# Loading expert weights in sixteen pieces inside the attention loop instead of two large transfers ahead of it

## The chip, the cores and the metric

The kernel runs on one core of one Trainium2 chip. The metric is the device time of one execution in microseconds (us), as the median of several runs.

## What is computed

One transformer block over 2048 tokens of width 128, in float32: an adaptive layer norm, sparse attention with 16 heads of 8 columns in which each head attends only to its 819 best-scored keys (40% of 2048), a second layer norm, and a feed-forward layer with 8 experts, of which each token uses one. Cut to what matters here:

```python
ga = (2 * (ga >= 0) - 1) * jnp.maximum(jnp.abs(ga), 0.25)        # gb likewise
h = _layernorm(x) * (1 + ca) + sa
x = x + ga * attention(h)          # per head: the top 819 keys by a routing score, softmax, weighted sum of values
h = _layernorm(x) * (1 + cb) + sb
logits = jnp.einsum('btd,ed->bte', h, router_w)
mask = jax.nn.one_hot(jnp.argmax(jax.nn.softmax(logits), axis=-1), 8)
u = jnp.square(jax.nn.relu(jnp.einsum('btd,edh->ebth', h, expert_fc)))
out_e = jnp.einsum('ebth,edh->ebtd', u, expert_proj)
x = x + gb * jnp.einsum('ebtd,bte->btd', out_e, mask)
```

The weights of the experts, `expert_fc` and `expert_proj`, are 2 MB each. They are used in the second half alone.

## The kernel before

Every engine has its own program, written out by hand, and semaphores order them; nothing is scheduled by a tool. The engines are PE (tensor engine: matmuls and transposes), DVE (vector engine), ACT (scalar engine), POOL (general engine) and SP, which here only issues transfers.

First the layer norm, the projections and the choice of keys for each head. A table of positions is built for this on DVE (lines 1000 and 1005). Its first stage, `B0`, lies in the memory that later holds the expert weights, `WE`, so the weights may only come in once the first five tables are done; SP waits for that on the semaphore `columns_ready`.

Then the attention loop. Heads go in 8 pairs, and each pair's 2048 queries in 4 chunks of 512, so there are 32 chunks, `n` = 0 to 31. Per chunk:
- PE makes scores for the maxima of a later chunk, in "units" of 128 queries by about 410 keys (lines 1437 to 1442), and DVE reduces each unit to its maximum (line 1067). The maxima are split into three bfloat16 parts (lines 1077 to 1084), PE turns them (`turn_m`, line 1456), ACT copies them to `MT` (line 764), and SP moves them with two small transfers, one for each head of the pair, into three rows of `QS` under the queries (`m_rows`, line 484). In this way the maxima are subtracted inside the score matmul. Each such transfer adds 16 to the semaphore `mrow`.
- PE starts a chunk only when its own rows are there: `pe.wait_ge(mrow, 32 * (n + 1))` on line 1543. It then makes the scores in seven steps (`scores`, line 1485), ACT takes the exponential of each step (line 791), and PE weighs the values with them (`weigh`, line 1501).
- The rows of chunk `n + 1` are turned in step 3 of chunk `n`, so their transfer is issued in the second half of chunk `n`.

At the head of every fourth chunk SP also loads the queries of the pair after the next (`load_q`, line 476, six transfers). POOL meanwhile gathers the keys and values of a coming pair from memory (line 562) and prepares them (lines 579 to 611); PE turns the prepared keys (`turn_k`, line 1450).

After the loop come the second layer norm, the routing, the sorting of tokens by expert, and 23 tiles of 128 tokens. For each tile DVE copies one expert's two weights out of `WE` (lines 1285 and 1291). Before the first of these copies it waits on `we_in`, the semaphore of the weight transfers.

All transfers that SP issues go through one queue. The part of it that the change touches:

```python
m_rows(0)
sp.wait_ge(columns_ready, AHEAD)
for n, w_part in enumerate((w_fc, w_proj)):
    sp.dma_start(WE[:, :, HD * n:HD * (n + 1)], w_part.rearrange("n p c -> p n c"))\
        .then_inc(we_in, 16)
for n in range(NCH):
```

Of the kernel before, what the change touches and what calls it, by code (L numbers as in the profile page):

```python
# [95 lines left out]
NE = 8  # L96
HD = 4 * E
# [56 lines left out]

def build(nc, x, w_q, w_kv, b_q, b_kv, w_r1, b_r1, w_r2, b_r2, c_col, wmod, w_route, w_fc, w_proj, const, out):
    _, at = constants()
    NCONST = const.shape[1]
    q_parts_dram = nc.dram_tensor("q_parts_dram", (H, PARTS, D, L), BF16, kind="Internal").ap()
# [3 lines left out]
    with ExitStack() as ctx:  # L162
        def sb(name, shape, dt=F32):
            return ctx.enter_context(nc.sbuf_tensor(name, shape, dt))
# [4 lines left out]
        def sem(name):  # L169
            return ctx.enter_context(nc.semaphore(name))  # L170
# [34 lines left out]
        WE = sb("WE", [P, NE, 2 * HD])  # L205
# [141 lines left out]
        we_in = sem("we_in")  # L347
# [104 lines left out]
        @block.sync  # L452
        def _(sp):
            for g in range(4):
                sp.dma_start(X[:, 4 * g:4 * g + 4, :], x_t[:, 4 * g:4 * g + 4, :]).then_inc(x_in[g], 16)
                if g == 1:
                    sp.dma_start(C[:, :], const).then_inc(const_in, 16)
            for dst, src in ((WR1, w_r1), (WR2S, w_r2), (BR1, b_r1), (BR2, b_r2), (WQ, w_q), (WKV, w_kv), (BQ, b_q),
                             (WROUTE, w_route)):
                sp.dma_start(dst[:, :], src).then_inc(w_in, 16)  # L460
            sp.dma_start(BG[:, :, :, :], b_kv).then_inc(bias_in, 16)

            for g in range(4):
                sp.wait_ge(kv_ready, 2 * g + 2)
                sp.dma_start(kv_t[:, 4 * g:4 * g + 4, :], KV[:, 4 * g:4 * g + 4, :]).then_inc(kv_out, 16)
            for part in range(PARTS):
                sp.wait_ge(q_ready, 4 * part + 4)
                sp.dma_start(q_parts_dram[:, part, :, :], QP[:, part, :]).then_inc(qparts_out, 16)
            sp.wait_ge(qparts_out, 16 * PARTS)
            sp.wait_ge(qs_zero, 2)  # L470

            def load_q(i):
                for e in range(2):
                    src = q_parts_dram[2 * i + e:2 * i + e + 1, :, :, :].rearrange("h a d l -> (h a d) l")
                    for row, k in ((0, 3), (3, 2), (5, 1)):
                        sp.dma_start(QS[64 * e + D * row:64 * e + D * (row + k), i % 2, :],
                                     src[0:D * k, :]).then_inc([qs_even, qs_odd][i % 2], 16)

            def m_rows(n):
                c = n % NQ  # L480
                sp.wait_ge(mt_ready, n + 1)
                for e in range(2):
                    dst = QS[64 * e + KROWS:64 * e + SROWS, n // NQ % 2, CHUNK * c:CHUNK * (c + 1)]
                    sp.dma_start(dst.rearrange("a (t q) -> a t q", q=P), MT[12 * e:12 * e + 12, n % 2, :])\
                        .then_inc(mrow, 16)

            load_q(0)
            load_q(1)
            m_rows(0)
            sp.wait_ge(columns_ready, AHEAD)  # L490
            for n, w_part in enumerate((w_fc, w_proj)):
                sp.dma_start(WE[:, :, HD * n:HD * (n + 1)], w_part.rearrange("n p c -> p n c"))\
                    .then_inc(we_in, 16)
            for n in range(NCH):
                if n % NQ == 0 and 1 <= n // NQ < NP - 1:
                    sp.wait_ge(st_filled, KSTEPS * n)
                    load_q(n // NQ + 1)
                if n + 1 < NCH:
                    m_rows(n + 1)


            for g in range(4):
                ts = slice(4 * g, 4 * g + 4)
                sp.wait_ge(x2_ready, 2 + g)
                sp.dma_start(rows_t[:, ts, E:2 * E], X2[:, ts, :]).then_inc(rows_out, 16)
                sp.wait_ge(xn2_ready, 4 * g + 4)
                sp.dma_start(rows_t[:, ts, 0:E], XN2[:, ts, :]).then_inc(rows_out, 16)
            sp.wait_ge(added, 16 * SLOT_TILES)
# [350 lines left out]
        def _(dve):  # L859
# [412 lines left out]
            dve.wait_ge(tail_step, next_tail())  # L1272
            v.scalar_tensor_tensor(owner[:, :], OWNER, -1.0, empty[:, :], ALU.add, ALU.add).then_inc(owner_ready, 1)  # L1273
            dve.wait_ge(tile_ready, 1)
            dve.wait_ge(we_in, 32)

            expert_reg = [dve.alloc_register("expert_even"), dve.alloc_register("expert_odd")]

            def load_expert(n):
                dve.reg_load(expert_reg[n % 2], TEI[0:1, n:n + 1])  # L1280
# [411 lines left out]
```

## Time and profile before

| | us |
|---|---|
| median of 3 timed runs | 525.98 |
| the three runs | 526.09, 525.98, 523.41 |
| span of the profiled execution, first to last instruction | 558.4 |
| busy in it: PE, DVE, ACT, POOL | 451.8, 396.4, 311.3, 217.7 |

The profiled execution has no time of its own besides its span, and the span is 32.4 us above the timed median; the rows and sums that follow are of the profiled execution. In the rows, PE is the tensor engine's matmuls, PEld its loading of the stationary operand (which runs beside PE), SPq the issuing of transfers by SP. `QS<-MT` is the transfer of the rows of maxima, `WE<-in_w_fc` and `WE<-in_w_proj` are the expert weights. A time in square brackets at a row's end is how long the engine stood idle before it, and what ended the idle time.

### The profile page before, as it was taken

How to read it: one execution, taken by the hardware profiler on the slowest of the kernel's cores; microseconds unless marked ns; L12 is line 12 of the kernel's file. 1: busy time of each engine (PE TensorE's matmuls, PEld its weight loads, DVE VectorE, ACT ScalarE, POOL GpSimd, SP SyncE). 2: the span in 40 equal slices, each digit the busy share in tenths (PEclk: the TensorE clock that was granted, in tenths of full speed). 3: DMA queues.
4: the chain of work that ended last, by engine and by line, in shares of the span. 5: the costliest groups of instructions: out<-in, count | busy, mean ns of one | idle time of the engine just before them, and what ended most of it. 6: DMA issues, size and time to landing. Idle time of an engine off the chain costs nothing.

```text
span 558.4 us, 9397 instructions
## 1 busy us (share of the span) xinstructions
PE 451.8 (81%) x3252; PEld 221.0 (40%) x3253; DVE 396.4 (71%) x1063; ACT 311.3 (56%) x457; POOL 217.7 (39%) x301
## 2 busy tenths in 40 slices
PE   4674754789999997998999899999999770769665
PEld 4341621223433432443434333333333270658564
DVE  8788864758986996787689668888889558134323
ACT  3435000357785785676578567778778740446333
POOL 3100576523414375266248425442003000655643
PEclk9878555569997999999799989999999955788878
DMA  7034300620100100100010010010000040211100
GB/s 230 0 126 118 82 6 6 217 90 4 32 2 6 33 3 5 30 6 6 3 32 3 6 32 2 6 33 2 2 2 0 22 133 0 76 41 42 44 17 12
DMA packets 20207, 21.11 MB, mean 38 GB/s; under 512 B 5740, under 2 KB 15792, under 8 KB 20160
## 3 DMA queue, kind: packets, MB, share of 16 engines
q1 hardware_dynamic: 14704, 16.12, 9.6%
q0 software_dynamic: 5168, 4.00, 3.9%
q8 instruction: 26, 0.43, 0.3%
q10 hardware_dynamic: 288, 0.39, 0.2%
q14 instruction: 21, 0.17, 0.1%
HBM read 14.41 MB, written 7.27 MB: 39 GB/s over the span
## 4 chain that ended last, share of the span: by engine, by line
PE 67%; DVE 16%; issue 7%; another core or an unknown queue 3%; DMA 2%; ACT 2%; POOL 1%; SPq 0%; POOLq 0%; DVEq 0%; ACTq 0%
PE OP L1501 17%; PE ST L1485 13%; PE ST L1461 6%; PE SC L1439 6%; PE SC L1437 6%; DVE tile_max L1067 5%; PE SC L1620 4%; PE ST L1631 3%; DVE PR L937 2%; PE OP L1509 2%; PE SC L1391 2%; DMA QS<-MT 2%; PE OP L1586 1%; PE SC L1441 1%
## 5 line engine op out<-in xcount | busy, mean ns | idle before, releaser
L1067 DVE TENSOR_REDUCE tile_max<-SC 128x1 f32<-128x410 f32 (+1 forms) x512 | 271.4, 577 | 74.9 <-PE SC L1437 49.2
L791 ACT ACTIVATE PR<-ST 128x1024 f32<-128x1024 f32 (+1 forms) x224 | 208.7, 962 | 62.4 <-PE ST L1485 57.0
L562 POOL DMA_INDIRECT G<-kv_dram,idx x104 | 106.8, 1027 | 169.0 <-ACT PR L791 108.8
L1485 PE MATMUL ST<-QS,KT 51*128 51x512 bf16 (+1 forms) x416 | 112.8, 403 | 3.6 <-DMA QS<-MT 2.7
L1501 PE MATMUL OP<-PR,VS 128*32 128x512 f32 x768 | 111.2, 653 | 0.4 <-ACT PR L791 0.4
L1437 PE MATMUL SC<-KT,QS 48*128 48x410 bf16 x256 | 80.6, 370 | 8.5 <-DVE tile_max L1067 4.5
L1485 PEld LDWEIGHTS ST<-QS,KT 51*128 51x128 bf16 (+1 forms) x416 | 30.2, 97 | 55.5 <-issue 39.3
L1439 PE MATMUL SC<-KT,QS 48*128 48x409 bf16 x128 | 47.3, 370 | 4.0 <-DVE tile_max L1067 1.1
L1441 PE MATMUL SC<-KT,QS 48*128 48x358 bf16 x128 | 43.4, 339 | 5.8 <-DVE tile_max L1067 3.7
L1620 PE MATMUL SC<-HT,PR 128*128 128x128 f32 x184 | 29.9, 316 | 18.3 <-issue 15.7
L686 POOL DMA_INDIRECT KV<-rows_dram,owner x23 | 24.3, 1054 | 50.5 <-DVE owner L1273 43.8
L1291 DVE COPY PR<-WE 128x512 f32 x23 | 10.4, 451 | 41.6 <-PE ST L1631 22.6
L838 ACT ACTIVATE HT<-ST,mod_col,one_cb 128x128 f32<-128x128 f32 x23 | 10.5, 457 | 52.1 <-PE ST L1611 31.2
L1461 PE MATMUL ST<-C,OS 128*128 128x32 f32 x248 | 38.8, 281 | 0.2
L1437 PEld LDWEIGHTS SC<-KT,QS 48*128 48x128 bf16 x256 | 19.3, 96 | 46.4 <-DVE tile_max L1067 30.4
L764 ACT ACTIVATE MT<-ST 24x128 bf16<-24x128 bf16 x32 | 8.5, 267 | 50.7 <-PE ST L1461 22.3
L1461 PEld LDWEIGHTS ST<-C,OS 128*128 128x128 f32 x248 | 32.2, 190 | 11.4 <-issue 10.7
L1620 PEld LDWEIGHTS SC<-HT,PR 128*128 128x128 f32 x184 | 27.1, 227 | 20.0 <-issue 17.0
L1439 PEld LDWEIGHTS SC<-KT,QS 48*128 48x128 bf16 x128 | 12.0, 94 | 57.5 <-DVE tile_max L1067 41.8
L695 POOL DMA_INDIRECT out<-PR,owner x23 | 23.3, 1015 | 26.6 <-DVE PR L1299 20.7
L618 POOL TENSOR_TENSOR XN<-OTS,REC 128x128 f32<-128x128 f32 x14 | 5.5, 413 | 61.2 <-DVE REC L1090 56.4
L1631 PE MATMUL ST<-PR 128*128 128x128 f32 x184 | 27.9, 300 | 0.3 <-issue 0.3
(257 smaller groups left out, 555.2 us busy)
## 6 DMA issues: line engine op xcount, KB each, us to landing
kv_dram<-KV SPq DMA_DIRECT2D x4, 512.0 KB, 2.9
WE<-in_w_fc SPq DMA_DIRECT2D x1, 2048.0 KB
WE<-in_w_proj SPq DMA_DIRECT2D x1, 2048.0 KB
G<-kv_dram,idx POOLq DMA_INDIRECT x104
q_parts_dram<-QP SPq DMA_DIRECT2D x3, 512.0 KB, 3.7
QS<-q_parts_dram SPq DMA_DIRECT2D x16, 96.0 KB
X<-in_x SPq DMA_DIRECT2D x4, 256.0 KB, 6.1
QS<-q_parts_dram SPq DMA_DIRECT2D x16, 64.0 KB
```

The lines of the kernel that those rows point to most:

```text
L562: pool.indirect_dma_start(G[:, i % 2, slot_of(s), :], None, kv_dram, bass.IndirectOffsetOnAxis(ap=idx[:, i, s:s + 1].bitcast(U32), axis=0) ...
L686: pool.indirect_dma_start(HS[:, n % NT, :], None, rows_dram, bass.IndirectOffsetOnAxis(ap=owner[:, n:n + 1].bitcast(U32), axis=0), bounds_ ...
L791: nc.scalar.activation(PR[:, k, 0:cols], ST[:, (KSTEPS * n + k) % 2, 0:cols], ACT.Exp, scale=float(D) ** -0.5).then_inc(exp_done, 1)
L1067: v.tensor_reduce(tile_max[:, n % 2, at_col:at_col + 1], bank(RING_AT["unit", u])[:, 0:410 - f], AX.X, ALU.max).then_inc(s_reduced, 1)
L1437: last = mm(to[:, 0:410], q, KT[rows, i % 2, 0:410], start=True, stop=True)
L1439: last = mm(to[:, 0:409], q, KT[rows, i % 2, 410:KEEP], start=True, stop=True)
L1441: mm(to[:, 0:358], q, KT[rows, i % 2, 410:768], start=True, stop=True)
L1461: last = mm(turned_o(n)[:, 32 * t:32 * t + 32], OS[:, P * t:P * t + P], cc("sum_groups"), start=True, stop=True)
L1485: last = mm(ST[:, at_step % 2, 512 * e:512 * e + 512], KT[rows, i % 2, P * tile:P * tile + P], QS[rows, i % 2, CHUNK * c:CHUNK * (c + 1)], ...
L1501: last = mm(OP[32 * g:32 * g + 32, :], VS[:, i % 2, tile, :], PR[:, k, 512 * e:512 * e + 512], start=first, stop=False, skip_group_check=True)
L1620: last = mm(SC[:, b, P * c:P * c + P], WFC[:, b, P * c:P * c + P], HT[:, P * n:P * n + P], start=True, stop=True)
L1631: last = mm(ST[:, b, 0:E], R2[:, b, P * c:P * c + P], WPROJ[:, b, P * c:P * c + P], start=(c == 0), stop=(c == 3))
```

## The change

The two transfers of 2 MB ahead of the loop go. In the loop, each of the chunks 0 to 15 issues one transfer of 256 KB (one expert's half: up or down projection) right after it has issued the rows of maxima of the next chunk. The wait for `columns_ready` stays where it was. DVE waits for sixteen landings instead of two.

```diff
             m_rows(0)
             sp.wait_ge(columns_ready, AHEAD)
-            for n, w_part in enumerate((w_fc, w_proj)):
-                sp.dma_start(WE[:, :, HD * n:HD * (n + 1)], w_part.rearrange("n p c -> p n c"))\
-                    .then_inc(we_in, 16)
+
+            def load_expert(piece):
+                at, half = piece // 2, piece % 2
+                sp.dma_start(WE[:, at, HD * half:HD * (half + 1)], (w_fc, w_proj)[half][at]).then_inc(we_in, 16)
+
             for n in range(NCH):
                 if n % NQ == 0 and 1 <= n // NQ < NP - 1:
                     sp.wait_ge(st_filled, KSTEPS * n)
                     load_q(n // NQ + 1)
                 if n + 1 < NCH:
                     m_rows(n + 1)
-
+                if n < 2 * NE:
+                    load_expert(n)
...
-            dve.wait_ge(we_in, 32)
+            dve.wait_ge(we_in, 16 * 2 * NE)
```

On SP's queue, at the start of the chunk loop, the order of issues changes as follows (`QS<-MT` is a pair of row transfers where it says x2, `QS<-q_parts_dram` are loads of queries, a count stands behind x):

```order
 L476 DMA QS<-q_parts_dram 16x2048
 L476 DMA QS<-q_parts_dram 8x2048
+L484 DMA QS<-MT 3x4x128 x4
+L494 DMA WE<-in_w_fc 128x512
 L484 DMA QS<-MT 3x4x128 x2
-L492 DMA WE<-in_w_fc 128x8x512
-L492 DMA WE<-in_w_proj 128x8x512
-L484 DMA QS<-MT 3x4x128 x8
+L494 DMA WE<-in_w_proj 128x512
+L484 DMA QS<-MT 3x4x128 x2
```

The rows of chunks 0 and 1 now follow each other directly, and the first piece of a weight stands behind the rows of chunk 1, the second behind those of chunk 2.

Further on in the loop, SP's queue over chunks 4 to 7, between two sets of query loads, shows what is new in a later group of chunks:

```order
 L476 DMA QS<-q_parts_dram 8x2048
-L484 DMA QS<-MT 3x4x128 x8
+L484 DMA QS<-MT 3x4x128 x2
+L494 DMA WE<-in_w_fc 128x512
+L484 DMA QS<-MT 3x4x128 x2
+L494 DMA WE<-in_w_proj 128x512
```

Four pairs of rows that stood in one run now each have a piece behind them. The order of the instructions on PE, DVE, ACT and POOL is the same in both kernels.

## Rows read from the trace of the kernel before

**Rows 1.** The page: span, and the chain that ended last by engine.

```profile
span 558.4 us, 9397 instructions
...
PE 67%; DVE 16%; issue 7%; another core or an unknown queue 3%; DMA 2%; ACT 2%; POOL 1%; SPq 0%; POOLq 0%; DVEq 0%; ACTq 0%
```

**Rows 2.** The chain, 96 to 135 us: start us, us, what.

```profile
100.79 1.85 DMA QS<-MT
...
102.69 0.95 PE ST L1485 x2
...
107.76 0.73 SPq L484
...
108.53 6.79 DMA QS<-MT
115.32 0.68 issue
116.00 1.25 PE ST L1485 x3
```

**Rows 3.** SP's timeline, 97 to 112 us.

```profile
101.58 0.42 SPq L492 DMA_DIRECT2D WE<-in_w_fc  x1
102.06 0.57 SPq L492 DMA_DIRECT2D WE<-in_w_proj  x1
107.76 1.47 SPq L484 DMA_DIRECT2D QS<-MT  x2
```

**Rows 4.** Stretches: us, busy us of each engine, clock share, DMA share, GB/s.

```profile
core 0: us, PE busy (x) PEld busy (x) DVE busy (x) ACT busy (x) POOL busy (x), PEclk, DMA share, GB/s
104.00:114.00 10.00, 9.88 (x52) 2.43 (x50) 7.73 (x18) 6.46 (x8) 3.05 (x3) 0.50 1.02 372
114.73:116.00 1.27, 0.00 (x1) 0.00 (x1) 0.00 (x0) 0.00 (x0) 0.96 (x1) 0.50 0.22 72
116.00:119.84 3.84, 3.84 (x19) 1.08 (x21) 2.06 (x4) 2.03 (x3) 0.15 (x1) 0.50 0.04 2
119.84:123.25 3.41, 3.04 (x25) 1.94 (x21) 2.88 (x8) 2.94 (x4) 0.85 (x1) 1.00 0.04 5
123.25:126.67 3.42, 3.42 (x19) 0.79 (x19) 1.15 (x3) 1.45 (x3) 1.00 (x1) 0.50 0.03 4
126.67:129.09 2.42, 2.42 (x24) 0.62 (x22) 2.40 (x5) 2.01 (x2) 0.28 (x1) 1.00 0.00 0
157.54:167.81 10.27, 9.79 (x86) 3.95 (x83) 8.84 (x21) 8.28 (x11) 1.85 (x3) 1.00 0.01 2
```

**Rows 5.** PE's timeline where chunk 0 ends and chunk 1 starts.

```profile
112.80 1.93 PE L1501 MATMUL OP<-PR,VS 128*32 128x512 f32 x8
116.00 0.61 PE L1485 MATMUL ST<-QS,KT 51*128 51x512 bf16 x1 [1.27 <-DMA QS<-MT]
```

**Rows 6.** ACT's and DVE's timeline, 97 to 128 us.

```profile
112.91 1.02 ACT L791 ACTIVATE PR<-ST 128x1024 f32<-128x1024 f32 x1 [0.74 <-PE ST L1485]
127.02 1.02 ACT L791 ACTIVATE PR<-ST 128x1024 f32<-128x1024 f32 x1 [1.62 <-PE ST L1485]
...
112.58 1.07 DVE L1067 TENSOR_REDUCE tile_max<-SC 128x1 f32<-128x409 f32 x2 [0.34 <-PE SC L1442]
```

**Rows 7.** SP: its waits (us, times, longest), and its timeline from 241 us.

```profile
SPq L484 <- ACT MT L764: 256.4, 26, 38.2
...
241.56 36.56 SPq L484 DMA_DIRECT2D QS<-MT  x8
```

**Rows 8.** DMA issues: count, size of each, median us to landing.

```profile
rows_dram<-X SPq DMA_DIRECT2D x4, 256.0 KB, 2.8
```

**Rows 9.** SP's and PE's timeline around the starts of chunks 2 and 4.

```profile
129.09 0.39 PE L1485 MATMUL ST<-QS,KT 51*128 51x512 bf16 x1
...
144.22 1.44 SPq L484 DMA_DIRECT2D QS<-MT  x2
146.89 2.24 SPq L476 DMA_DIRECT2D QS<-q_parts_dram  x6
...
148.06 0.39 PE L1485 MATMUL ST<-QS,KT 51*128 51x512 bf16 x1
```

**Rows 10.** POOL's, SP's and PEld's timeline around the last gather of pair 3.

```profile
195.31 1.00 POOL L562 DMA_INDIRECT G<-kv_dram,idx  x1 [0.96 <-ACT PR L791]
198.93 0.62 POOL L579 TENSOR_TENSOR G<-G,BG 128x208 f32<-128x208 f32 x1 [2.63 <-DMA G<-kv_dram,idx]
...
195.69 1.48 SPq L484 DMA_DIRECT2D QS<-MT  x2
...
202.95 0.24 PEld L1450 LDWEIGHTS SC<-identb,KS 128*128 128x128 bf16 x4 [0.58 <-POOL RS L596]
```

**Rows 11.** Line 1285, the copies out of the expert weights.

```profile
L1285 DVE COPY PR<-WE x23: 419/422/654, 473.2 to 547.6; 128x512 f32 x23
```

## The prediction

> **What bounds the kernel now.** I read the chain that ended last first. Two thirds of it is the tensor engine [rows 1], so a change matters only where that engine is made to wait or let go earlier. The change touches one queue, SP's, so I then followed the chain in order of time over the start of the chunk loop. Here the reader is to see one piece that is out of line: the row transfer of chunk 0 takes 1.85 us from its issue to its landing, the one of chunk 1 takes 6.79, and both are followed directly by the tensor engine's score matmuls [rows 2]. SP's own timeline says why: between the two pairs of row transfers it issues the two weight transfers of 2 MB, at 101.58 and 102.06 [rows 3]. The table of stretches says that from 104 to 114 us the 16 DMA engines are full (share 1.02, 372 GB/s) [rows 4]. So the rows of chunk 1, issued behind them from 107.76, land only when the 4 MB are through, at 108.53 + 6.79 = 115.32.
>
> What that costs is read from the tensor engine alone. Its last work of chunk 0, the weighing of line 1501, starts at 112.80 and lasts 1.93, to 114.73; the first score matmul of chunk 1 starts at 116.00, with 1.27 us of idle time put down to the row transfer [rows 5]. In those 1.27 us no engine but POOL does anything [rows 4]: the last exponential of chunk 0 has ended at 112.91 + 1.02 = 113.93 and the last maximum at 112.58 + 1.07 = 113.65 [rows 6], so both wait for the tensor engine and nothing else holds chunk 1 back.
>
> **The base of the sum.** The profiled execution spans 558.4 us, 32.4 us more than the timed median of 525.98. The rows do not say where those 32.4 us lie. I make the sum in microseconds against the span and subtract the same number from 525.98, because the wait is the difference between a transfer's landing and the end of one chunk, both near 115 us; what that choice can cost stands among the rivals.
>
> **Part 1: the 4 MB leave the place ahead of the loop.** The second row transfer of chunk 1 is then issued about 108.53 as before, on an empty queue. Chunk 0's took 1.85 us [rows 2], so it lands near 110.4, 4.3 us before the tensor engine asks at 114.73. The wait goes as a whole: -1.27 us. It is not refilled at that spot, since exponentials and maxima are done 0.8 and 1.1 us before 114.73.
>
> How much of 1.27 reaches the end depends on the clock. The tensor engine runs at the lower of its two levels, 1.2 GHz (0.50), through chunk 0 and the first 3.84 us of chunk 1; it then has 3.41 us at 2.4 GHz (1.00), 3.42 at 1.2 and is back at 2.4 [rows 4]. If the clock rises as long after the start of chunk 1 as now, the whole 1.27 is kept. If it rises at the same time of the execution as now, 1.27 us more of chunk 1 run at half speed, and the gain is 0.64. These are the two ends for this term; I take 1.27, because the rise comes after the tensor engine resumes and not before, though it had been busy for nearly all of 104 to 114 (9.88 of 10.00 us).
>
> Does chunk 0 also get faster without the transfer beside it? The exponential of 128x1024 takes 1.02 us at 112.91 under full DMA and 1.02 at 127.02 without [rows 6]. I take nothing.
>
> **Part 2: sixteen pieces of 256 KB, each behind a pair of row transfers.** SP has the time: it spends 256.4 us waiting for the copied maxima [rows 7], and a weight issue takes 0.42 to 0.57 us [rows 3]. A piece moves in 262144 B / 372 GB/s = 0.70 us at the rate of rows 4, and a 256 KB transfer of this kernel lands 2.8 us after its issue [rows 8]. The next rows come one chunk later, about 10 us (chunk 5 spans 10.27) [rows 4], so a piece has left the queue long before. The piece stands behind its own rows, never ahead of them. How tight those rows are: for chunk 4 the pair is issued from 144.22 for 1.44 us, hence the second at about 144.94, landing near 146.8 by the 1.85 of rows 2, and the tensor engine needs it at 148.06 [rows 9]: 1.26 us to spare. Between nothing and 0.70 us of sharing, both inside 1.26, I take nothing. The six loads of q at the head of every fourth chunk follow a piece by several microseconds (146.89 in rows 9) and are not needed at once.
>
> The gathers on POOL use the same 16 DMA engines. The last gather of pair 3 is issued at 195.31, its preparation starts at 198.93 after a wait of 2.63 us, and the tensor engine's transposes wait for its end until 202.95 [rows 10]. This is the one tight place. Bounds: nothing, if the gather lands before the piece moves, and 0.7 us, once, if it gives way to a whole piece. The rows of that chunk go out from 195.69 for 1.5 us, so the piece is issued near 197.2, when the gather is nearly in. I take nothing.
>
> **Part 3: the later end of the weights.** The last piece goes out behind the rows of chunk 16, in an SP run of four pairs that ends at 241.56 + 36.56 = 278.12 [rows 7]; the first read of the weights is at 473.2 [rows 11]. The cover is some 195 us, and the larger count that is waited for costs nothing.
>
> **Sum.** -1.27 + 0 + 0 = -1.3 us. On the span 557.1; on the timed median 525.98 - 1.3 = 524.7. Its own range, by the clock (-0.64) and by a timed execution whose chunk 0 runs 526/558 as long (12.04 becomes 11.35, so the wait is 2.0): 524.0 to 525.3. That is 0.25%, about half of the 0.5% that a measurement of this kernel can tell from no change (its three runs lie 2.7 us apart).
>
> **The rivals.**
> *B, the clock comes back with the wait (faster).* Chunk 1 takes 129.09 - 116.00 = 13.09 us, of which 7.26 at 1.2 GHz; chunk 5, with the same transposes of keys but wholly at 2.4, takes 10.27 [rows 4, 9]. Were chunk 1 like chunk 5, another 2.8 us come back: 525.98 - 1.27 - 2.82 = 521.9. For it: the rise does follow the resumption. Against it: 12 busy microseconds of chunk 0 raised nothing, and the clock falls again inside chunk 1 with no wait of this kind. I give it 0.17. The Trainium skill (TensorE: Matmul & The Clock Gate, HAM oscillation — how this bites in real kernels) holds that waits for transfers between bursts of matmuls put the engine back to its slow clock and that work fed without such waits keeps it fast; by that rule B would be the forecast, 521.9 in place of 524.7. The trace agrees in part: the rise follows the end of the wait, but the low stretch before it held no such waits.
>
> *C, the wait is longer when nothing is profiled (faster).* If chunk 0 took chunk 5's 10.27 us in a timed execution instead of 102.69 to 114.73 = 12.04 [rows 2, 5], the tensor engine would arrive 1.8 us earlier against the same landing, and 1.27 + 1.77 = 3.04 us would go: 522.9. Nothing shown speaks for that clock there: 0.09.
>
> *D, the clock stays low longer (slower).* Chunk 1's 3.41 us at 2.4 GHz hold 3.04 us of tensor work, which at 1.2 GHz costs 3.04 more; a further chunk like chunk 0 instead of chunk 5 costs 1.8. -1.27 + 3.04 + 1.77 = +3.5: 529.5. It decides against the change when more than 1.27 us of work that now runs at 2.4 GHz falls back to 1.2: 0.06.
>
> *E, the rows land late behind pieces (slower).* If a row pair shared the queue such that it came 2.8 us later, 1.5 us would stand open in each of the 16 chunks: +25 - 1.3, some 550. It decides from 1.26 us of delay on. Against it: the rows go first, and the previous piece is some 10 us older. I give it 0.04. The Trainium skill (DMA: Bandwidth & Descriptors, Bandwidth) speaks against small transfers, asking for 1 MiB or more in each; by the fixed 2.0 us and 436 GB/s of its anatomy section, a piece is an estimated 2.6 us, near the row's 2.8, and would be hidden too.
>
> *F, nothing to see.* The gain is eaten by the tight gather or by later changes of the clock: 526.0. Against it stands only how small 1.3 us is: 0.11.
>
> **Numbers.** The forecast holds 0.53. Faster by over 0.5%: B and C, 0.26. Slower: D and E, 0.10. Within: the rest, 0.64. The range goes down to B, 521.8, and up past F by half the spread of the three runs, 527.3; D and E and the far tails are left out.
>
> **What would show it.** In the changed profile the rows of chunk 1 land about 1.9 us after their issue, the tensor engine goes from line 1501 of chunk 0 to line 1485 of chunk 1 without idle time, and no chunk up to 16 shows a new wait for the row transfer; DMA shows a short burst in each of these chunks. Step 1 is wrong if a wait for an exponential or a maximum stands at that spot; step 2, if waits for rows appear in chunks 2 to 16 or the transposes of pair 3 wait longer than 0.6 us. A time below 523 says that the clock moved; one above 528, that chunks were held up.

## The result: 0.73% faster, by more than forecast and by another wait

The changed kernel takes 520.1 us (median of 20 runs) beside 524.38 us for the kernel before (20 runs, timed together with it): a ratio of 0.9927 with a 95% interval of 0.9908 to 0.9947, so 2.8 to 4.8 us less. The ratios leave out executions over 1.5% above the fastest of their kernel, so they are not exactly the quotient of the two medians. The forecast was 1.3 us less, with 521.8 as the lower end of its range. The direction was right, the size was about three times as large, and the time lies below the range.

One plain fact has to stand first, since the forecast can't be understood without it: the execution from which [rows 1 to 11] were taken was a disturbed one. In all later profiles the span is about 1.8 us under the time of the same run, so a span of 558.4 us belongs to a run of some 560 us. Of the 20 runs only one, of 563.17 us, is anywhere near; the other 19 lie between 520 and 529.

The page of the changed kernel has a span that fits its time (this run took 519.37 us), and the same shares by engine as [rows 1], but POOL now has 6% of the chain:

```profile
span 517.6 us, 9413 instructions
...
PE 66%; DVE 16%; issue 7%; POOL 6%; DMA 3%; ACT 1%; POOLq 0%; DVEq 0%; ACTq 0%
```

SP's timeline of the changed kernel, against [rows 3]: the rows of chunks 0 and 1 go out in one run, the first piece behind them, and each later pair has a piece behind it.

```profile
92.05 9.45 SPq L484 DMA_DIRECT2D QS<-MT  x4
101.55 0.42 SPq L494 DMA_DIRECT2D WE<-in_w_fc  x1
112.60 1.46 SPq L484 DMA_DIRECT2D QS<-MT  x2
114.10 0.42 SPq L494 DMA_DIRECT2D WE<-in_w_proj  x1
```

The chain of the changed kernel, 85 to 130 us, is where the surprise stands. Where [rows 2] had a transfer of rows, the chain now runs through POOL: its last gather for head pair 1 lands 2.42 us after its issue, is prepared (lines 582 to 614; each number is 3 higher than in the kernel before), and the first weighing of chunk 0 follows at once.

```profile
93.72 2.42 DMA G<-kv_dram,idx
...
96.21 0.64 POOL G L582
...
100.56 0.20 POOL VS L614
...
100.90 1.94 PE OP L1504 x8
```

At the start of chunk 1, which answers to [rows 5], the tensor engine's timeline shows no idle time between the last weighing of chunk 0 and the first scores of chunk 1, as forecast:

```profile
105.16 1.07 PE L1504 MATMUL OP<-PR,VS 128*32 128x512 f32 x8
106.16 0.39 PE L1488 MATMUL ST<-QS,KT 51*128 51x512 bf16 x1
```

And the stretches that answer to [rows 4] (the columns are the same): chunk 0 at the lower clock, 1.37 us of it at the higher, and chunk 1 whole at the higher in 10.27 us.

```profile
94.84:104.79 9.95, 9.40 (x47) 2.80 (x49) 7.32 (x17) 5.74 (x7) 6.35 (x18) 0.50 0.09 30
104.79:106.16 1.37, 1.37 (x14) 0.26 (x11) 1.15 (x3) 0.92 (x2) 1.07 (x2) 1.00 0.08 6
106.16:116.43 10.27, 9.79 (x85) 3.96 (x83) 8.52 (x20) 8.41 (x12) 3.55 (x5) 1.00 0.14 31
```

By these alone it could be that the wait is gone and the clock came back. So the first need was an ordinary profile of the kernel before.

### The profile page after: what moved, and what is told of

Its sections match the earlier page's. It is cut to its first block, busy times and chain, and to the rows that moved or that the text cites. A ratio compares the mean times of both kernels' runs of the same rounds, so it can differ in the third digit from the quotient of the medians.

```text
span 517.6 us, 9413 instructions
## 1 busy us (share of the span) xinstructions
PE 440.4 (85%) x3253; PEld 213.0 (41%) x3253; DVE 395.7 (76%) x1063; ACT 311.1 (60%) x457; POOL 216.9 (42%) x301
## 4 chain that ended last, share of the span: by engine, by line
PE 66%; DVE 16%; issue 7%; POOL 6%; DMA 3%; ACT 1%; POOLq 0%; DVEq 0%; ACTq 0%
PE OP L1504 19%; PE ST L1488 12%; PE ST L1464 7%; PE SC L1442 6%; DVE tile_max L1070 5%; PE SC L1440 4%; POOL G L565 4%; PE ST L1634 3%; PE SC L1623 3%; PE OP L1512 2%; DMA KV<-rows_dram,owner 2%; DVE PR L940 2%; PE OP L1589 1%; PE ST L1394 1%; PE ST L1459 1%
## 5 line engine op out<-in xcount | busy, mean ns | idle before, releaser
L1070 DVE TENSOR_REDUCE tile_max<-SC 128x1 f32<-128x410 f32 (+1 forms) x512 | 271.1, 576 | 54.9 <-PE SC L1440 51.6
L565 POOL DMA_INDIRECT G<-kv_dram,idx x104 | 105.5, 1015 | 148.5 <-ACT PR L794 88.7
L1488 PE MATMUL ST<-QS,KT 51*128 51x512 bf16 (+1 forms) x416 | 109.3, 401 | 1.8 <-DMA QS<-MT 1.5
L1504 PE MATMUL OP<-PR,VS 128*32 128x512 f32 x768 | 108.8, 640 | 0.7 <-ACT PR L794 0.4
L1464 PEld LDWEIGHTS ST<-C,OS 128*128 128x128 f32 x248 | 32.2, 190 | 11.4 <-issue 10.7
L1623 PE MATMUL SC<-HT,PR 128*128 128x128 f32 x184 | 25.9, 288 | 0.0
L1634 PE MATMUL ST<-PR 128*128 128x128 f32 x184 | 25.1, 279 | 0.4 <-issue 0.4
L1445 PE MATMUL SC<-KT,QS 48*128 48x51 bf16 x128 | 24.6, 192 | 0.0
```

Of the source, the lines that this page charges most:

```text
L565: pool.indirect_dma_start(G[:, i % 2, slot_of(s), :], None, kv_dram, bass.IndirectOffsetOnAxis(ap=idx[:, i, s:s + 1].bitcast(U32), axis=0) ...
L1070: v.tensor_reduce(tile_max[:, n % 2, at_col:at_col + 1], bank(RING_AT["unit", u])[:, 0:410 - f], AX.X, ALU.max).then_inc(s_reduced, 1)
L1464: last = mm(turned_o(n)[:, 32 * t:32 * t + 32], OS[:, P * t:P * t + P], cc("sum_groups"), start=True, stop=True)
L1488: last = mm(ST[:, at_step % 2, 512 * e:512 * e + 512], KT[rows, i % 2, P * tile:P * tile + P], QS[rows, i % 2, CHUNK * c:CHUNK * (c + 1)], ...
L1504: last = mm(OP[32 * g:32 * g + 32, :], VS[:, i % 2, tile, :], PR[:, k, 512 * e:512 * e + 512], start=first, stop=False, skip_group_check=True)
L1623: last = mm(SC[:, b, P * c:P * c + P], WFC[:, b, P * c:P * c + P], HT[:, P * n:P * n + P], start=True, stop=True)
```

## The experiments

Three theories stood: **Q**, the rows of chunk 1 stand behind the 4 MB in SP's queue (the forecast's wait, larger than it looked); **S**, the 4 MB share the 16 DMA engines with POOL's last gathers of pair 1, whose preparation the first weighing waits for; **L**, the gain lies in other stretches. They were timed in four sets, each on a chip of its own with the kernel before beside it, whose medians lay between 524.3 and 525.2 us; runs of different sets are compared by their ratios.

| run | median, us | ratio to the kernel before (95%) | from the issue of chunk 0's rows to its first weighing, us |
|---|---|---|---|
| before, second profile | 525.26 | 1.0007 (0.9969 to 1.0045) | 13.2 |
| before, third profile | 524.81 | 1.0021 (0.9985 to 1.0057) | 13.4 |
| changed, the result above | 520.1 | 0.9927 (0.9908 to 0.9947) | 8.9 |
| changed, again | 520.37 | 0.9921 (0.9877 to 0.9965) | 8.9 |
| 2 x 2 MB behind the rows of chunk 1 | 521.1 | 0.9896 (0.9838 to 0.9954) | 8.7 |
| 2 x 2 MB on ACT's queue | 524.49 | 0.9984 (0.9948 to 1.002) | 12.7 |
| 2 x 2 MB behind the loop's rows | 518.47 | 0.9856 (0.9805 to 0.9907) | 8.8 |
| the same, again | 519.88 | 0.9903 (0.9871 to 0.9934) | 8.8 |
| sixteen pieces ahead of the loop | 520.92 | 0.9942 (0.9901 to 0.9982) | 10.1 |
| 2 x 2 MB after pair 1's gathers landed | 527.5 | 1.0073 (1.0036 to 1.0109) | 8.7 |
| 2 x 2 MB ahead of the rows of chunk 0 | 520.85 | 0.9967 (0.9928 to 1.0007) | 8.8 |
| 1 MB ahead of the loop, 3 MB behind it | 522.54 | 1.0004 (0.9965 to 1.0043) | 11.8 |
| changed, POOL held up 4.2 us | 523.77 | 0.9996 (0.9962 to 1.0029) | 12.8 |

The last column is the start of the first weighing (line 1501 in the kernel before) minus the start of SP's first row issue of chunk 0, both from the run's profile. In the first profile it was 8.4 us. The edits shift the line numbers in some runs: the weighing is line 1501, 1502, 1504 or 1511.

### The kernel before, profiled again

No edit.

> The kernel before, unchanged, for a second profile of it, since the first one spans 558.4 us and the timed median is 524.4. Theory Q (queue): the rows of chunk 1 stand behind the 4 MB in SP's queue, and what that costs the tensor engine at the start of chunk 1 is larger in an ordinary execution than the 1.27 us read from the first profile: 3 to 4 us of wait there, and the lower clock lasts beyond it. Theory S (shared engines): the wait there is 1.3 us or less, and the 4 MB instead delay POOL's last gathers of pair 1 by 2 us or more, so that the first weighing of chunk 0 waits for POOL. Theory L (elsewhere): neither is above 1.3 us, and the 4 us lie in other stretches of the clock. All: 524 us, ratio 1.00.

Its profile, of a run of 528.99 us, showed the wait of S (4.78 us at the first weighing) and none of Q (the scores of chunk 1 start with no idle time before them):

```profile
106.19 1.93 PE L1501 MATMUL OP<-PR,VS 128*32 128x512 f32 x8 [4.78 <-POOL VS L611]
...
112.61 0.60 PE L1485 MATMUL ST<-QS,KT 51*128 51x512 bf16 x1
```

Since that run was one of the longer ones, a third was taken:

> The kernel before once more, for a third profile, since the second one was of one of its longer executions. Theory S: the last gather of pair 1 lands 4 to 7 us after its issue and the first weighing of chunk 0 waits 2.5 us or more for POOL; the rows of chunk 1 are not waited for. If the second profile was the exception: the gather lands within 3 us. 524 to 525 us.

The third is of a run of 520.2 us and shows the same. POOL's timeline: the last gather is issued at 93.77, its data are waited for until 100.80, and the preparation ends with line 611 at 105.33. PE's timeline: the scores of chunk 0 start at 94.95, the first weighing only at 105.47, after 4.90 us of idle time put down to POOL, and chunk 1 starts at 110.56 with no wait at all.

```profile
93.77 1.00 POOL L562 DMA_INDIRECT G<-kv_dram,idx  x1 [0.30 <-issue]
100.80 0.62 POOL L579 TENSOR_TENSOR G<-G,BG 128x208 f32<-128x208 f32 x1 [6.03 <-DMA G<-kv_dram,idx]
...
105.14 0.19 POOL L611 COPY VS<-G 64x8 f32<-64x8 f32 x1
...
94.95 0.60 PE L1485 MATMUL ST<-QS,KT 51*128 51x512 bf16 x1 [1.52 <-DMA QS<-MT]
105.47 1.94 PE L1501 MATMUL OP<-PR,VS 128*32 128x512 f32 x8 [4.90 <-POOL VS L611]
...
110.56 0.39 PE L1485 MATMUL ST<-QS,KT 51*128 51x512 bf16 x1
```

Why the first weighing, which is of pair 0, waits for a gather of pair 1 stands in POOL's program (lines 625 to 629 of the kernel before; `prep` prepares a pair's keys, `prep_v` its values):

```python
gathers(1)
prep(1)
pool.wait_ge(prepared0, 2)
prep_v(0)
prep_v(1)
```

POOL works in this order, so the values of pair 0, which the weighing needs, come behind the keys of pair 1, which need the last gather. To put `prep_v(0)` ahead of `prep(1)`, and to drop its own wait for the prepared keys (line 600), would be another remedy to look into; it was not tried.

SP's timeline of that run says what lies beside the gather: the two weight transfers are issued within half a microsecond of it.

```profile
92.11 1.66 SPq L484 DMA_DIRECT2D QS<-MT  x2
93.81 0.42 SPq L492 DMA_DIRECT2D WE<-in_w_fc  x1
94.28 0.57 SPq L492 DMA_DIRECT2D WE<-in_w_proj  x1
```

In the first profile the same gather had escaped. There POOL was on time (issue at 94.88, preparation at 97.34), but the maxima were late, so that the weights went out at 101.58 [rows 3], when the preparation was done:

```profile
94.88 1.00 POOL L562 DMA_INDIRECT G<-kv_dram,idx  x1 [0.30 <-issue]
97.34 0.62 POOL L579 TENSOR_TENSOR G<-G,BG 128x208 f32<-128x208 f32 x1 [1.46 <-issue]
```

What made the maxima late is not known. From the last copy of keys (line 757) to the turned maxima of chunk 0, the tensor engine took 6.5 us in the third profile (85.04 to 91.51) and 13.2 us in the first (86.14 to 99.29), with longer idle times between the last units on it and on DVE. One of these, of 1.44 us, ends with nothing on this core ("remote" in the list of waits). The profile has 21 such idle times, 55 us in all; no other profile has one. But the other 20 come after chunk 0's rows were issued, and the two largest groups stand behind the loop: they belong to the length of the span, not to the late maxima.

```profile
98.48 0.58 DVE L1067 TENSOR_REDUCE tile_max<-SC 128x1 f32<-128x410 f32 x1 [1.44 <-remote]
...
ACT HT L838 <- remote: 19.2, 5, 4.9
DVE PR L1291 <- remote: 18.9, 6, 4.8
DVE tile_max L1067 <- remote: 8.4, 5, 2.3
```

### The place alone: whole transfers behind the rows of chunk 1

```diff
-            for n, w_part in enumerate((w_fc, w_proj)):
-                sp.dma_start(WE[:, :, HD * n:HD * (n + 1)], ...)
             for n in range(NCH):
...
                     m_rows(n + 1)
+                if n == 0:
+                    for half, w_part in enumerate((w_fc, w_proj)):
+                        sp.dma_start(WE[:, :, HD * half:HD * (half + 1)], ...)
```

> The two transfers of 2 MB stay whole, but are issued behind the rows of chunk 1 instead of ahead of them. Theory Q: the rows of chunk 1 land 1.9 us after their issue and those of chunk 2, about 10 us later, find at most the last 1 or 2 us of the 4 MB ahead of them: 520 us, as with sixteen pieces (ratio 0.992). Theory S: 520 us too, since the gathers of pair 1 are in by then. Theory L, or if the small pieces themselves matter: 524 us.

521.1 us, a ratio of 0.9896. Sixteen pieces are not needed for the gain; moving the two whole transfers behind one more pair of rows, to 102.42 us, gives it. The gather lands in time (the preparation starts at 97.00) and the weighing waits 0.23 us. This does not yet tell Q from S.

### The queue alone: the same time, ACT's queue

```diff
-            sp.wait_ge(columns_ready, AHEAD)
-            for n, w_part in enumerate((w_fc, w_proj)):
-                sp.dma_start(WE[:, :, HD * n:HD * (n + 1)], ...)
...
             copy_mt(0)
+            act.wait_ge(columns_ready, AHEAD)
+            for half, w_part in enumerate((w_fc, w_proj)):
+                act.dma_start(WE[:, :, HD * half:HD * (half + 1)], ...)
```

> The two transfers of 2 MB are issued by ACT at the same time as before (right after the first copy of maxima), so that they share the 16 DMA engines with the rows of chunk 1 and the gathers as before, but are in another queue. Theory Q: the rows of chunk 1 go past them and land within 3 us: 520 to 521 us. Theory S: the gathers are as late as before: 523 to 524.5 us.

524.49 us: nothing gained. That is the time S forecast and not Q's, but it was reached by another path. The weights now go out 0.3 us ahead of the rows of chunk 0 instead of behind them, and the second of those two transfers takes 6.05 us, though only its twin stands ahead of it in SP's queue:

```profile
92.26 0.86 SPq L484
...
93.17 6.05 DMA QS<-MT
```

The scores of chunk 0 wait for these rows, and the first weighing then follows them without a wait:

```profile
99.27 0.61 PE L1485 MATMUL ST<-QS,KT 51*128 51x512 bf16 x1 [5.69 <-DMA QS<-MT]
...
104.91 1.93 PE L1501 MATMUL OP<-PR,VS 128*32 128x512 f32 x8
```

The gather is late too (POOL waits 4.80 us for it), but pair 0's values are ready at 104.24, before they are needed. So the 12.7 us of this run are those of the rows. It shows that a queue of its own did not protect a small transfer here, and says nothing of what the late gather alone costs. Against Q speak the two profiles of the kernel before, in which nobody waits for the rows of chunk 1.

### No weights in the loop

```diff
                     m_rows(n + 1)
-
+            for half, w_part in enumerate((w_fc, w_proj)):
+                sp.dma_start(WE[:, :, HD * half:HD * (half + 1)], ...)
```

(and the two transfers ahead of the loop gone).

> The two transfers of 2 MB are issued behind the last rows of the loop, so that no weights move in it until chunk 30; they have some 40 us until their first use. Theories Q and S: 520 us as with the pieces, and a time below 519 would mean that the pieces in the loop cost something of their own. Theory L: between 520 and 524 by chance of the clock.

518.47 us, the lowest median of the first set, as if the pieces cost 1.6 us. These few runs also had a higher mean granted clock (0.877, against 0.871 for the changed kernel). The two were then timed side by side:

> The changed kernel beside the next one, on one chip. Theory S: 520 us, the last gather of pair 1 within 2.6 us, no wait for POOL above 0.5 us at the first weighing.

> All weights behind the last rows of the loop, once more, on the same chip as the changed kernel. If the pieces in the loop cost something of their own, 518.5 us, 1 to 2 us below the changed kernel; if the first difference between the two was chance, 520 us, the same as it.

520.37 and 519.88 us, with intervals that overlap almost wholly (0.9877 to 0.9965 and 0.9871 to 0.9934). In the changed kernel the gather is in use 2.5 us after its issue and the weighing waits 0.34 us, as S forecast. No cost of the pieces in the loop can be told from chance, and no version tried here is shown to beat the changed kernel.

### The size alone: sixteen pieces ahead of the loop

```diff
-            for n, w_part in enumerate((w_fc, w_proj)):
-                sp.dma_start(WE[:, :, HD * n:HD * (n + 1)], ...)
+            for piece in range(2 * NE):
+                at, half = piece // 2, piece % 2
+                sp.dma_start(WE[:, at, HD * half:HD * (half + 1)], (w_fc, w_proj)[half][at]).then_inc(we_in, 16)
...
-            dve.wait_ge(we_in, 32)
+            dve.wait_ge(we_in, 16 * 2 * NE)
```

> Sixteen transfers of 256 KB as in the changed kernel, but all of them ahead of the loop, where the two of 2 MB stood. Theory S (the weights share the 16 DMA engines with POOL's last gathers of pair 1, whose preparation the first weighing of chunk 0 waits for): the place decides and not the size, 524 to 526 us, with the last gather of pair 1 landing some 6 us after its issue. If the size of a transfer decides: 520 us.

A miss: 520.92 us, most of the gain, with the pieces in the old place. S survives in a weaker form. SP issues a piece every 0.47 us and the first one at 94.84, just after the gather (94.81), so when the gather moves, only some of the 4 MB are under way; POOL waits for it, but less, and the weighing waits 1.67 us instead of 4.90:

```profile
98.53 0.62 POOL L579 TENSOR_TENSOR G<-G,BG 128x208 f32<-128x208 f32 x1 [2.73 <-DMA G<-kv_dram,idx]
...
103.22 1.94 PE L1501 MATMUL OP<-PR,VS 128*32 128x512 f32 x8 [1.67 <-POOL VS L611]
```

That the place decides and not the size was wrong as I put it. The reading that fits is that it counts how much has been issued while the gather moves; this run alone does not show it, the next one is a second point.

### A smaller dose: 1 MB

```diff
-            for n, w_part in enumerate((w_fc, w_proj)):
-                sp.dma_start(WE[:, :, HD * n:HD * (n + 1)], ...)
+            sp.dma_start(WE[:, 0:4, 0:HD], w_fc[0:4].rearrange("n p c -> p n c")).then_inc(we_in, 16)
...
+            sp.dma_start(WE[:, 4:, 0:HD], ...)        # behind the loop's rows
+            sp.dma_start(WE[:, :, HD:], ...)
...
-            dve.wait_ge(we_in, 32)
+            dve.wait_ge(we_in, 48)
```

> A smaller dose: 1 MB of the weights (half of the up projections) stays ahead of the rows of chunk 1, the other 3 MB go behind the last rows of the loop. 1 MB takes 2.8 us at 372 GB/s. Theory S: the last gather of pair 1 is 1 to 2.8 us late and the first weighing with it, so 1 to 2.8 of the 5 us stay: 520.5 to 522 us, against 518.5 with all 4 MB behind the loop. If only the whole 4 MB hold anything up: 518.5 us.

522.54 us, just above the expected range, and a ratio of 1.0004, which reaches from a gain of 0.35% to a loss of 0.43%. The median lies 1.8 us under that of the kernel before beside it (524.32), so the time leaves open how much of the gain is lost. The profile is clearer: the first weighing comes 11.8 us after the rows' issue, against 8.8 with no weights there and 13.3 with 4 MB, so a quarter of the bytes keeps two thirds of the delay. The gather is in use 5.5 us after its issue instead of 2.3 to 2.5, some 3 us more, which is about what 1 MB takes by itself (2.8 us at 372 GB/s), and the weighing waits 3.35 us.

```profile
100.32 0.61 POOL L579 TENSOR_TENSOR G<-G,BG 128x208 f32<-128x208 f32 x1 [4.46 <-DMA G<-kv_dram,idx]
...
104.98 1.94 PE L1501 MATMUL OP<-PR,VS 128*32 128x512 f32 x8 [3.35 <-POOL VS L611]
```

### The gather spared, the rows not

```diff
             sp.wait_ge(columns_ready, AHEAD)
+            sp.wait_ge(gathered, 16 * STEPS)
             for n, w_part in enumerate((w_fc, w_proj)):
```

> The two transfers of 2 MB stay ahead of the rows of chunk 1, but SP waits first until the gathers of pair 1 have landed (about 97 us). Theory S: the last gather lands within 2.5 us and the first weighing of chunk 0 starts near 101 instead of 106 us. Then chunk 0 ends near 106 us, while the rows of chunk 1, behind 4 MB that now end near 111 us, are late by 4 to 5 us, so that theory Q's wait appears at last: 523 to 525 us, with that wait in the profile. If the rows' queue never mattered: 520 us.

527.5 us, 0.7% slower than before and above the expected range. This run shows that Q's wait is real, but covered in the ordinary kernel before: with the gather in time the weighing starts at 102.08 after a wait of 0.25 us, and now the rows of chunk 1, behind 4 MB that were issued some 3 us later, are waited for.

```profile
102.08 1.93 PE L1502 MATMUL OP<-PR,VS 128*32 128x512 f32 x8 [0.25 <-POOL VS L612]
111.87 0.60 PE L1486 MATMUL ST<-QS,KT 51*128 51x512 bf16 x1 [4.56 <-DMA QS<-MT]
```

The wait that goes (4.90 to 0.25 us) and the one that comes (4.56) nearly cancel, so they don't explain a time that is longer by 0.7%, some 3.8 us. The profile shows what was added: the clock had risen to 2.4 GHz at 105.75 us, fell back to 1.2 at 109.16, within the new wait, and over the 22 us from the end of that wait (111.87) the mean granted clock was 0.83. In the third profile of the kernel before, whose wait lies in a stretch at 1.2 GHz, it was 1.00 over the first 22 us of chunk 1.

### Both spared: whole transfers earlier

```diff
-            m_rows(0)
             sp.wait_ge(columns_ready, AHEAD)
+            sp.wait_ge(gathered_late, 16 * (STEPS - EARLY))
             (the two transfers of 2 MB)
+            m_rows(0)
```

> The two transfers of 2 MB are issued ahead of the rows of chunk 0, as soon as the gathers of pair 0 have landed (about 80 us); by the 14 us from issue to last packet in the second profile of the kernel before they are through near 94 to 95 us, when the last gather of pair 1 is being issued. Theory S: that gather lands within 3 us and the first weighing is not held: 519 to 521 us. If whole transfers ahead of the loop cost time wherever they stand: 524 us.

520.85 us, within the expectation; its ratio of 0.9967 has an interval that just touches 1, so by time alone this is not shown to be faster. In the profile the gather and the weighing are as in the changed kernel (the preparation starts 2.5 us after the last gather's issue, the weighing waits 0.33 us). Whole transfers ahead of the loop hold up neither, if they are through before a small one is waited for.

### The late preparation alone

```diff
             gathers(1)
+            pool.wait_ge(gathered, 16 * STEPS)
+            for n, rows in enumerate((2 * NT, 2 * NT, NT)):
+                shape = [P, rows, CODES]
+                nc.gpsimd.tensor_tensor(held[:, n, 0:rows, :], key_of[...], cc("code")..., ALU.subtract)
             prep(1)
```

(`held` is a part of `HT` that nothing reads at that time.)

> The changed kernel, whose weights don't disturb the gathers, but POOL does two and a half idle subtractions of 128x896 (1.69 us each in the first profile) between the landing of pair 1's gathers and their preparation; their result goes to memory that nothing reads. This holds the preparation up by about 4.3 us with no transfer involved. Theory S: the first weighing of chunk 0 waits about 4.6 us for POOL as in the kernel before, and the whole gain is gone: 524 to 525 us. If the late preparation is not what costs (but the full DMA engines are, or the place in the queue): 520 to 521 us.

523.77 us and a ratio of 0.9996: with the weights in pieces in the loop, but the preparation late by 4.2 us, no gain is left that can be told from chance. The median of 523.77 is a little under the expected range and 1.0 us under that of the kernel before beside it. The wait at the weighing was 3.38 us, less than the 4.6 expected, because the tensor engine itself came 1 us later: beside POOL's idle work DVE took 0.84 us for a step in the splitting of the maxima (line 1091 here) that takes 0.19 in the changed kernel, and the turning waited 1.13 us for it. That delay is hidden by the longer wait behind it, so the first weighing is still POOL's. With this L is out: the pieces in the loop are those of the changed kernel, and only the preparation was moved.

```profile
97.17 4.22 POOL L633 TENSOR_TENSOR HT<-key_of,C 128x896 f16<-128x896 f16 x3 [1.32 <-DMA G<-kv_dram,idx]
...
106.02 1.93 PE L1511 MATMUL OP<-PR,VS 128*32 128x512 f32 x8 [3.38 <-POOL VS L614]
```

## Why the prediction was wrong

**The step that failed is the base of the sum**: "I make the sum in microseconds against the span and subtract the same number from 525.98, because the wait is the difference between a transfer's landing and the end of one chunk, both near 115 us." The 32.4 us between span and median were seen, and taken to be harmless. In that execution the rows of chunk 0 were issued 5.0 us after POOL's last gather of pair 1 (99.88 against 94.88), in the ordinary ones 1.7 us before it, so that the gathers were in before the weights went out. The wait that the forecast removed, 1.27 us at chunk 1, is in neither ordinary profile of the kernel before; the wait that the change removes, 4.78 and 4.90 us at the first weighing, is not in the profile that the forecast read. That the forecast had the direction right was in part luck: its wait and the one removed both come from the 4 MB, but by different paths.

**Part 1** said the rows of chunk 1 would be waited for no more: true in the changed profile, but true in the second and third profiles of the kernel before as well. The run with the gather spared shows that the mechanism is real where the late gather doesn't hide it (4.56 us).

**Part 2** costed the gathers at nothing, with 0.7 us, once, as the upper bound, and looked at pair 3 alone. The bound was the time of one piece; what a gather loses beside a full set of DMA engines was measured as 1.2 us beside pieces issued one by one, 3 us beside 1 MB and 4.5 us beside 4 MB. For the change itself the step came out right: POOL's waits for gathers sum to 11.4 us in the changed kernel and to 11.3 with all weights behind the loop, and no version without them in the loop was faster beyond chance.

**Part 3** held: no wait for the weights' landing shows.

**The sum**, with what was measured: from the issue of chunk 0's rows to the first weighing 13.2 and 13.4 us before, 8.9 and 8.9 after, so 4.4 us, of which the timing shows 3.8 (2.8 to 4.8).

**The rivals.** B, the clock: its time was near the one measured, but its reason was not the one. In the third profile of the kernel before chunk 1 runs wholly at the higher clock in 10.27 us, as in the first of the changed kernel; in the second profile of each kernel the first 2 us or so of chunk 1 are at the lower one (2.3 and 1.9 us). So no clock came back there that one kernel has and the other lacks. The low stretch that the forecast took to hold no wait for a transfer had begun at 51.6 us, and the wait of 1.48 us for the rows of chunk 0 lies in it. C said the wait would be longer in a timed execution; the number was near, but the wait was another one. F, D and E did not come about; in the changed profile the tensor engine waits for rows 1.5 us once, at chunk 0, as before.

**Still open.** How the measured 3.8 us divide between the earlier weighing and what the clock does after it was not separated within an execution. One pair of profiles shows the trouble: the first weighing is 4.6 us earlier in the first profile of the changed kernel than in the third of the kernel before, the last weighing of the loop only 1.1 us, since after its rise the clock granted in the loop had a mean of 0.95 there and of 0.97 in the other. Over many runs the clock is not what separates the kernels. A straight line through the time and the mean granted clock of 109 runs of the kernel before in these sets puts, at equal clock, the changed kernel 3.1 to 3.6 us below it, the version with all weights behind the loop 3.4 to 3.7 us below, and the one with POOL held up level with it (an estimate; the removed wait lies at the lower clock and so raises the mean itself). At the single clock of 0.872, for example, six runs of the kernel before took 521.45 to 524.59 us and six of the changed kernel 519.38 to 521.39. What made the first profile's maxima late stays open too.

## What to carry to other kernels

If a profile's span does not fit the timed median, take another profile before reading any wait from it: stages that run beside each other may stand in another order in it. A large transfer is to be judged by every small transfer that someone waits for while it moves, on any queue, and not only by what stands behind it in its own; place it where no such transfer is in flight, or issue it in pieces spaced out in time. Ask also what stands behind the wait in the waiting engine's own program: here values whose gathers had landed some 20 us before waited behind keys whose last gather had not. When one such wait is removed, look for the one that it covered: here a queue of its own left the time where it was, and sparing the gather alone made it worse.

## What the runs showed of the hardware

A gather of one tile took 2.3 to 2.5 us from issue to the start of the work that waits for it when the DMA engines were nearly idle, 3.7 us beside pieces of 256 KB issued every 0.47 us, 5.5 us beside 1 MB, and 6.9 to 7.0 us beside 4 MB. A row transfer (3 KB, the second of its pair) took 1.85 us in an idle moment [rows 2] and 6.05 us beside 4 MB issued from ACT 0.3 us earlier.

The Trainium skill (DMA: Bandwidth & Descriptors, Issuing engines are not separate DMA queues) says that transfers from different engines run on the same 16 DMA engines and interleave. The runs agree, with these numbers: the gather did not have to wait for the end of the 4 MB (it was in at 100.8, while the second weight landed 14.3 us after its issue at 94.28, so near 108.6), but lost 4.5 us all the same.

In every profile the granted clock was at 1.2 GHz when chunk 0 began and rose only in chunk 0 or 1: 8 to 19 us after the first scores of chunk 0, and, the first profile apart (11.6 us), 2.3 to 8.7 us after the first weighing. In the first profile of the changed kernel the engine ran 9.95 us of chunk 0 at 1.2 GHz, busy for 9.40 of them, before the rise. The place of the rise differs between profiles of one kernel as much as between kernels.
